# Attention scores formed a second time, already turned, with one reciprocal of the sum for a pair of heads

## The reference

```python
scale, shift = split(cond @ W_emb + b_emb)        # one row per batch
xn  = rms_norm(x) * g_norm * (1 + scale) + shift
q, k, v = split(xn @ W_qkv)                       # 16 heads of 64
q, k = rms_norm(q) * g_q, rms_norm(k) * g_k       # over the 64 of a head
attn = softmax(q @ k.T * 64 ** -0.5)              # 512 x 512 per head
o = attn @ v
out = x + o + o @ W_out
```

## Time and profile before

| what | value |
|---|---|
| median of three runs | 2278.25 us |
| the profiled execution | 2278.89 us |
| its span | 2276.0 us |
| TensorE busy | 2256.2 us (99%) |
| VectorE busy | 1597.9 us (70%) |
| ScalarE busy | 1345.7 us (59%) |
| GpSimd busy | 651.7 us (29%) |
| granted TensorE clock | 0.999 |

### The profile page before, as it was taken

One profiled execution on the slowest core, in us unless ns is written; L12 is line 12 of the kernel. 1 busy time (PEld: TensorE's weight loads), 2 busy tenths in 40 slices (PEclk: granted clock), 3 DMA queues, 4 the chain that ended last, 5 costly groups with the idle time before them and its releaser, 6 DMA issues.

```text
span 2276.0 us, 36733 instructions
## 1 busy us (share of the span) xinstructions
PE 2256.2 (99%) x13392; PEld 2110.3 (93%) x13392; DVE 1597.9 (70%) x3284; ACT 1345.7 (59%) x3101; POOL 651.7 (29%) x880
## 2 busy tenths in 40 slices
PE   8999999999999999999999999999999999999999
PEld 4999989999999999999999999999999999999999
DVE  4898784787827778287872878738786487854875
ACT  4687772667616676176762667526674366743663
POOL 3444431324213241122312234122331223302220
PEclk9999999999999999999999999999999999999999
DMA  9544346422364332733236332362323723246331
GB/s 359 224 167 177 112 154 228 178 99 110 118 220 184 107 115 88 256 148 112 111 114 256 112 112 112 122 253 107 112 112 130 291 92 118 82 151 246 111 121 65
DMA packets 71269, 346.35 MB, mean 152 GB/s; under 512 B 7601, under 2 KB 43441, under 8 KB 47537
## 3 DMA queue, kind: packets, MB, share of 16 engines
q1 hardware_dynamic: 71088, 344.01, 41.2%
HBM read 293.65 MB, written 50.33 MB: 151 GB/s over the span
## 4 chain that ended last, share of the span: by engine, by line
PE 86%; DVE 8%; ACT 2%; issue 1%; POOL 0%; DMA 0%; ACTq 0%; DVEq 0%
PE proj_bank L502 18%; PE proj_bank L500 18%; PE proj_bank L501 18%; PE flip_bank L598 9%; PE pv_bank L609 5%; PE pv_bank L610 5%; PE score_bank L590 4%; PE score_bank L591 4%; PE flip_bank L553 2%; DVE probs L865 2%; DVE neg_max L859 2%; DVE pt_lo L869 2%; PE flip_bank L563 1%; ACT k_hi L700 1%; PE proj_bank L525 1%
## 5 line engine op out<-in xcount | busy, mean ns | idle before, releaser
L500 PE MATMUL proj_bank<-w_split,xn_hi 128*128 128x384 f32 x2048 | 700.0, 342 | 1.4 <-DVE res L907 0.8
L502 PE MATMUL proj_bank<-w_split,xn_lo 128*128 128x384 f32 x2048 | 688.5, 336 | 0.0
L501 PE MATMUL proj_bank<-w_split,xn_hi 128*128 128x384 f32 x2048 | 687.4, 336 | 0.0
L718 ACT ACTIVATE probs<-score_bank,neg_max 128x512 f32<-128x512 f32 x512 | 352.6, 691 | 213.5 <-DVE neg_max L859 211.2
L500 PEld LDWEIGHTS proj_bank<-w_split,xn_hi 128*128 128x128 f32 x2048 | 385.2, 188 | 18.1 <-DVE xn_lo L854 1.0
L501 PEld LDWEIGHTS proj_bank<-w_split,xn_hi 128*128 128x128 f32 x2048 | 385.5, 188 | 15.2
L724 ACT CAST pt_hi<-flip_bank 128x512 fp32r<-128x512 f32 x512 | 288.8, 591 | 182.0 <-PE flip_bank L598 91.1
L869 DVE TENSOR_TENSOR pt_lo<-flip_bank,pt_hi 128x512 fp32r<-128x512 f32 x512 | 339.9, 685 | 78.1 <-ACT pt_hi L724 75.9
L502 PEld LDWEIGHTS proj_bank<-w_split,xn_lo 128*128 128x128 f32 x2048 | 384.8, 188 | 0.0
L859 DVE TENSOR_REDUCE neg_max<-score_bank 128x1 f32<-128x512 f32 x512 | 341.3, 684 | 17.0 <-PE score_bank L591 13.0
L865 DVE TENSOR_SCALAR probs<-probs,row_inv 128x512 f32<-128x512 f32 x512 | 275.7, 539 | 18.1
(11 more groups left out here) (86 smaller groups left out, 3205.1 us busy)
## 6 DMA issues: line engine op xcount, KB each, us to landing
w_split<-w_store SPq DMA_DIRECT2D x140, 1536.0 KB, 7.0
w_store<-w_split SPq DMA_DIRECT2D x20, 1536.0 KB, 10.1
x_tile<-in_x SPq DMA_DIRECT2D x32, 512.0 KB, 11.0
w_raw<-in_w_qkv SPq DMA_DIRECT2D x16, 768.0 KB, 8.4
w_split<-w_store SPq DMA_DIRECT2D x12, 1024.0 KB, 5.1
w_raw<-in_x SPq DMA_DIRECT2D x56, 192.0 KB, 6.7
out<-w_raw SPq DMA_DIRECT2D x56, 192.0 KB, 1.9
emb_stage<-in_w_emb SPq DMA_DIRECT2D x5, 1024.0 KB, 10.6
```

The source lines that it names most:

```text
L500: nc.tensor.matmul(dst, a_hi, w_hi, start=(kt == 0), stop=False)
L501: nc.tensor.matmul(dst, a_hi, w_lo, start=False, stop=False)
L502: mm = nc.tensor.matmul(dst, a_lo, w_hi, start=False, stop=(kt == KT - 1))
L718: nc.scalar.activation(probs[h][:, i, :], score_bank[n % 2][:, :], ACT.Exp, bias=neg_max[:, n:n + 1], accum_out=row_sum[:, n:n + 1]).then_ ...
```

## The change

The probabilities are no longer turned. Once the maxima of a head's rows are known, the scores are formed again with keys on the rows and queries on the columns (`F`), and the exponential is taken from that bank. The maximum of a query is now a value per column, so it is subtracted inside the product: `H` turns the 128x4 maxima with one transpose, VectorE spreads them over a diagonal of four rows in `q_max` (below the head's high part of q, which the new step `Z` copies there), and four rows of `k_lo` are set to one. The first scores (`S`), which serve for the maxima alone, lose their second matmul.

The exponential is written unscaled to `probs`, `E` copies its high part and `F` on VectorE subtracts it, both from SBUF. The sum of a column is over keys, that is over rows: GpSimd adds the four tiles of a head (`U`, three additions), ScalarE and VectorE bring the two heads together (`U`, `N`), `J` splits the sum, and `G` multiplies it with a matrix of ones. ScalarE takes the logarithm and the exponential of its negative, and VectorE scales the pair's result with this inverse and one Newton step. The flip banks now have one release counter for each engine that frees them. Three pairs are started early instead of two, and the first batch has two residual tiles instead of three. All five orders are new.

```diff
-LATE = 2
+LATE = 3
 HEAD, BODY, TAIL: all lists new; TensorE's part around pair 7 in BODY, for instance:
+        6F5 6W3 6F6 6F7 6W4 7T0 7T1 6W5 8C8 8C9 8C10 8C11 7S0 7S1 6W6 8C12 6W7 7S2 8C13 8C14 7S3 8C15 7H0 7S4 7S5 9C0
+        7F0 7F1 9C1 7S6 7S7 7F2 6G0 9C2 7H1 9C3 7W0 7W1 7F3 9C4 9C5 7F4 7F5 7W2 7W3 7F6 7F7 9C6 8T0 7W4 8T1 7W5 9C7 9C8
 ...and VectorE's:
+        6O0 7S1 6O1 8M2 7S2 7S3 6N0 7H0 6N1 8D3 7S4 7S5 6J0 8M3 7S6 7S7 7F0 7F1 6G0 7H1 9D0 7F2 7F3 7F4 7F5 7O0 9M0 8T0
 TensorE
                     elif kind == "S":
-                        pe.wait_ge(exp_done, it * 8 + (n - 2 + 1 + CREDIT))
+                        wait_past(pe, max_done, it * 8 + (n - 1))
...
-                        nc.tensor.matmul(score_bank[n % 2][:, :], q_t, k_hi[h][:, :], start=True, stop=False)
-                        nc.tensor.matmul(score_bank[n % 2][:, :], q_t, k_lo[h][:, :], start=False,
-                                         stop=True).then_inc(score_full, 1)
+                        nc.tensor.matmul(score_bank[n % 2][:, :], q_split[:, h, i * P:(i + 1) * P], k_hi[h][:, :],
+                                         start=True, stop=True).then_inc(score_full, 1)
+                    elif kind == "H":
+                        flip_wait(pe, u)
+                        pe.wait_ge(max_done, it * 8 + 4 * n + 4)
+                        nc.tensor.transpose(flip_bank[flip][0:TT, 0:P], neg_max[:, 4 * n:4 * n + 4],
+                                            ident[:, :]).then_inc(flip_full, 1)
                     elif kind == "F":
-                        for qt in range(TT):
-                            mm = nc.tensor.transpose(flip_bank[flip][:, qt * P:(qt + 1) * P],
-                                                     probs[h][:, qt, i * P:(i + 1) * P], ident[:, :])
+                        if i == 0:
+                            freed(pe, "H", h, it)
+                            freed(pe, "T", 1, it)
+                            pe.wait_ge(q_copied, it + 1)
+                        nc.tensor.matmul(flip_bank[flip][:, :], k_hi[h][:, i * P:(i + 1) * P], q_split[:, h, :],
+                                         start=True, stop=False)
+                        nc.tensor.matmul(flip_bank[flip][:, :], k_lo[h][:, i * P:(i + 1) * P], q_max[:, h, :],
+                                         start=False, stop=True).then_inc(flip_full, 1)
+                    elif kind == "G":
+                        pe.wait_ge(sum_lo_done, it + 1)
+                        nc.tensor.matmul(flip_bank[flip][:, :], head_ones[:, :], sum_hi, start=True, stop=False)
+                        nc.tensor.matmul(flip_bank[flip][:, :], head_ones[:, :], sum_lo, start=False,
+                                         stop=True).then_inc(flip_full, 1)
 ScalarE
+                    elif kind == "Z":
+                        for head in range(2):
+                            op = nc.scalar.copy(q_max[rows(head), head, :], f32(q_split[rows(head), head, :]))
+                    elif kind == "G":
+                        nc.scalar.activation(sum_inv, flip_bank[flip][:, :], ACT.Ln).then_inc(ln_done, 1)
+                        act.wait_ge(ln_done, it + 1)
+                        nc.scalar.activation(sum_inv, sum_inv, ACT.Exp, scale=-1.0).then_inc(inv_done, 1)
-                        nc.scalar.activation(probs[h][:, i, :], score_bank[n % 2][:, :], ACT.Exp,
-                                             bias=neg_max[:, n:n + 1],
-                                             accum_out=row_sum[:, n:n + 1]).then_inc(exp_done, 1)
                     elif kind == "F":
+                        nc.scalar.activation(probs[h][:, i, :], flip_bank[flip][:, :],
+                                             ACT.Exp).then_inc(flip_freed["ScalarE"], 1)
+                    elif kind == "E":
+                        nc.scalar.copy(pt_hi[n % 2][:, :], probs[h][:, i, :]).then_inc(p_hi_done, 1)
+                    elif kind == "U":
+                        nc.scalar.copy(key_moved[mine, :], probs[n][other, 3, :]).then_inc(keys_moved, 1)
+                    elif kind == "J":
+                        nc.scalar.copy(sum_hi, key_sum).then_inc(sum_hi_done, 1)
 VectorE
+                    elif kind == "H":
+                        nc.vector.tensor_tensor(q_max[at:at + TT, n, :].rearrange("p (t q) -> p t q", q=P),
+                                                flip_bank[flip][0:TT, 0:P].unsqueeze(1).to_broadcast([TT, TT, P]),
+                                                ident[0:TT, 0:TT].unsqueeze(2).to_broadcast([TT, TT, P]),
+                                                ALU.mult).then_inc(flip_freed["VectorE"], 1)
+                    elif kind == "F":
+                        nc.vector.tensor_tensor(pt_lo[n % 2][:, :], probs[h][:, i, :], f32(pt_hi[n % 2][:, :]),
+                                                ALU.subtract).then_inc(p_lo_done, 1)
                     elif kind == "N":
-                        nc.vector.reciprocal(row_inv[:, n:n + 1], row_sum[:, n:n + 1]).then_inc(inv_done, 1)
-                        nc.vector.tensor_scalar(probs[h][:, i, :], probs[h][:, i, :], row_inv[:, n:n + 1], None,
-                                                ALU.mult).then_inc(probs_ready, 1)
+                        nc.vector.tensor_tensor(key_sum[mine, :], probs[n][mine, 3, :], key_moved[mine, :],
+                                                ALU.add).then_inc(key_sum_done, 1)
+                    elif kind == "J":
+                        nc.vector.tensor_tensor(sum_lo, key_sum, f32(sum_hi), ALU.subtract).then_inc(sum_lo_done, 1)
+                    elif kind == "G":
+                        nc.vector.tensor_tensor(sum_times_inv, flip_bank[flip][:, :], sum_inv,
+                                                ALU.mult).then_inc(flip_freed["VectorE"], 1)
+                        nc.vector.scalar_tensor_tensor(o_pair[:, :], o_pair[:, :], -1.0, sum_inv, ALU.mult,
+                                                       ALU.mult).then_inc(o_scaled, 1)
+                        nc.vector.scalar_tensor_tensor(o_pair[:, :], sum_times_inv, -2.0, o_pair[:, :], ALU.add,
+                                                       ALU.mult).then_inc(o_norm_done, 1)
 GpSimd, three additions for each head as they come ready
+            def add_keys(it, n):
+                head, part = n // 3, n % 3
...
+                op = nc.gpsimd.tensor_tensor(e[:, dst, :], e[:, src, :], e[:, dst, :], ALU.add)
 tiles
-        first_res = [sb(f"res{i}", [P, QKV]) for i in range(3)]
+        first_res = [sb(f"res{i}", [P, QKV]) for i in range(2)]
```

More of the change, by code:

```diff
@@ L41 @@
[L41 to L45, removed]
@@ L226, in flip_buf, with order_of, flip_table @@
-def flip_buf(order, kind, n, p):
-    places = HEAD_FLIPS if order is HEAD else TAIL_FLIPS if order is TAIL else BODY_FLIPS
-    before = 0 if order is HEAD else HEAD_FLIPS[1]
-    assert BODY_FLIPS[1] % 2 == 0
-    return (before + places[0][(kind, n, p)][0]) % 2
-FIRST_X = {HEAD_FLIPS[0][("X", r, 0)][0] for r in range(TT)}
-def releases(order, u):
-    return u if order is HEAD and u - 2 in FIRST_X else u - 1
+def order_of(b):
+    return HEAD if b == 0 else TAIL if b == B - 1 else BODY
+def flip_table():
+    table, releases, counts = {}, [], {"ScalarE": 0, "VectorE": 0}
+    for b in range(B):
+        for step in order_of(b)["TensorE"]:
+            p, d, kind, n = read_step(step)
+            if kind in "TFXHG":
+                table[(kind, n, b + d if kind == "X" else b * PAIRS + p)] = len(releases)
+                for owner in ("VectorE", "ScalarE") if kind == "X" else ("ScalarE",) if kind == "F" else ("VectorE",):
+                    counts[owner] += 1
+                    releases.append((owner, counts[owner]))
+    return table, releases
@@ L243, in is_first @@
+FLIPS, RELEASES = flip_table()
 def is_first(b):
@@ L333, in cond_attention @@
         v_stage = sb("v_stage", [P, 2, TT, P])
-        q_split = [sb(f"q_split{h}", [P, T], F32R) for h in range(2)]
+        q_split = sb("q_split", [P, 2, T], F32R)
+        q_max = sb("q_max", [P, 2, T], F32R)
         k_hi = [sb(f"k_hi{h}", [P, T], F32R) for h in range(2)]
@@ L337, in cond_attention @@
         v_split = [sb(f"v_split{h}", [P, TT, P], F32R) for h in range(2)]
-        probs = [sb(f"probs{h}", [P, TT, T]) for h in range(2)]
+        probs = [sb("probs0", [P, TT, T])]
+        with nc.sbuf_tensor("sum_split", [P, TT, T], F32R) as sum_split:
+            pass
+        probs.append(sb("probs1", [P, TT, T]))
         pt_hi = [sb(f"pt_hi{i}", [P, T], F32R) for i in range(2)]
@@ L557, in cycle @@
                         for half in range(2):
-                            wait_past(pe, flip_free, releases(order, u + half))
+                            flip_wait(pe, u + half)
                             if half == 0:
@@ L721, in cycle @@
                     elif kind == "F":
                         act.wait_ge(flip_full, u + 1)
[L723 to L724 removed]
+                        if i == 0 and not is_first(it):
```

(17 more changed lines are left out.)

445 lines of the change are left out of this document (238 added, 207 removed).

## The result

| | before | after |
|---|---|---|
| median | 2278.01 us | 2401.78 us |
| the profiled execution's span | 2276.0 us | 2397.6 us |
| granted TensorE clock | 0.999 | 0.992 |

The ratio is 1.054, with a 95% interval from 1.053 to 1.056: the changed kernel is 124 us slower, where 35 us faster was forecast. The forecast was wrong, outside its range.

A forecast was written before the change was run, and what follows sets the result against it. The prediction took TensorE, busy 99% of the span, as the bound, so the span is the sum of what it issues. -63 + 14 + 6 + 5 + 3 = -35 us gave 2243 us, range 2216 to 2275 us.

The forecast's parts named there:

- the rival of the reloaded tables: If the logarithm needs another set, each pair has two table loads in `G`'s chain: 2357 us, chance 6%.
- The forecast case without reloads: Whole kernel: TensorE's saving less some waits gives 2243 us; the case, 2225 to 2262 us, had 64%.
- TensorE's own work: TensorE's matmuls and transposes, gained and lost in `S`, `F`, `G` and `H`, sum to -63 us.
- the sum of the waits: Waits that reach TensorE in four places: 14, 6, 5 and 3 us.
- Middle and later batches: 57 pairs: blocked VectorE operations exceed the spare time behind the maxima and before `F3`, 0.25 us per pair, 14 us.
- First batch: VectorE, nearly full there, becomes the bound for some pairs: 6 us, between 0 and 15.
- End of the first batch with two residual tiles: Tile 9 waits for a later load, tiles 10 and 11 load one and two round trips later: 5 us, 0 to 10.
- The end: The last pair's new chain, about 13 us, against about 11 us of other TensorE work: 3 us, between 0 and 5.
- The lock at the maxima: GpSimd's additions block VectorE in nearly every pair, late to `H` and `G`'s bank: 115 us, 2344 us in all, chance 10%.
- Other engines: Busy sums outside TensorE, none the bound: VectorE near 1760 us, ScalarE 1521 us, GpSimd near 1160 us.

The follow-up runs named there:

- experiment 1: The changed kernel with one activation table set holding both logarithm and exponential, loaded once at ScalarE's start: 2303.95 us, ratio 1.011 to the kernel before.
- experiment 7: experiment 1 without the Newton step, one multiplication in place of three VectorE operations, ScalarE's logarithm freeing the bank: 2302.55 us, ratio 1.011.
- experiments 1 and 4: experiment 1, and the same with GpSimd's additions cut to 4 of 512 columns: 2303.95 us and 2286.71 us.
- experiments 5 to 10: experiment 1 with steps moved, 2312.02 us; kernel before with reloads, 2349.94; no Newton step, whole or 4-column sums, 2302.55, 2286.60; copy or subtraction cut, 2293.92, 2283.91.

## Why the prediction was wrong

- **The step that failed: the rival of the reloaded tables, at 6%.** Its mechanism and place were right: two loads in `G`'s chain for each pair, the held bank, TensorE behind it. Its size was 2 us per pair, 128 us less 14; measured are 98 us, 1.5 us per pair. The forecast's own sum had no term for it: what failed was the chance. Nothing in the trace of before spoke against it, and I leaned on a rule. The Trainium skill, in "ScalarE activation tables: per-element evaluation and per-set limits", section "Table sets in the compiler and the runtime", has the loads placed per block by the greedy longest run. I took that to mean one set for the whole loop; the trace has 129 loads, so that reading does not hold for this kernel. The Trainium skill, in "ScalarE: Activation LUTs", section "Table sets: the hidden batching unit", counts one load for a logarithm followed by an exponential; it came true only in the experiments that load that set by its number, and the changed kernel itself has two loads for the two functions.
- **The forecast case without reloads, 2243 us: measured 2304 us.** Its size was off too, by 61 us. TensorE's own work was right: by the second sum it fell from 2213 to 2152 us, by 61 us where 63 were forecast. The single terms agree. `S`, by the starts of its matmuls, went from 248.2 to 132.9 us (-115.3, forecast -118.5), `G` takes 32.5 us (forecast 29.6), and an `H` 0.03 us from its start to the next one's and 0.08 on the interval behind it, the 0.11 that I had taken. So the step that failed in this case is the sum of the waits: +28 us forecast, +88 measured (112 less 24).
- **The waits of TensorE, by place.** Of the 88 us, 70 stand ahead of a step (87 less 17) and 18 inside steps, for which the forecast had no term. About 8 of these 18 are on the interval right behind a stall, 0.1 us longer than the typical one in `F` and `W`, 3 at the lower clock, and the other 7 are spread in small pieces. The 70:
  - Middle and later batches: 14 forecast, about 45 measured (49.8 and 3.9, less 8.4 and 0.1). This is the term that was mis-sized most. I had looked at the place behind the maxima, and the waits for `q_max` are small (2.6 us in experiment 1). The largest stalls are before the products `6W2` and `6W4` (16.6 us), where VectorE has `+X3 8D1` ahead of the subtractions, and at `3T0` (4.4 us); the rest is spread over many steps. I found the tight place by reading two spots of the lists and never went through those where x is turned.
  - First batch: 6 forecast; about 20 measured besides its end (33.2 less 8.2 and 5). And its cause was not the one named: VectorE with 73 us less in all changes it by 2 us (experiment 7).
  - End of the first batch with two residual tiles: 5 forecast, 5.0 measured. The chain of the changed kernel, which answers to the earlier trace rows, has the second round trip:
```profile
413.61 5.14 DMA out<-res
...
419.14 4.52 DMA out<-res
423.68 8.32 DMA res<-in_x
...
432.10 0.44 DVE res L988
```
  - The end: 3 forecast, 1.3 measured before `P3` in experiment 1 (2.6 after).
- **The lock at the maxima, at 10%,** was wrong in size. The subtraction is blocked as forecast, but what reaches TensorE from all of GpSimd's additions is 17 to 19 us, and not 115. VectorE itself loses 1.5 us per pair (1730.0 less 1636.2 us busy in experiments 1 and 4, over 64), where 2.6 were forecast.
- **Other engines:** ScalarE with one table has 1531.5 us (forecast 1521). The exponential out of a bank, without a bias from a tile and without the accumulator, takes 598 ns, not 691 and 200. That the sum is right within 11 us is luck: 512 exponentials are 48 us shorter, which I had not counted, and the accumulator's read had begun 0.11 us before the exponential's end, so that 56 of its 102 us were never ScalarE's to save.

So the 124 us are: 98 for the reloads, 17 for GpSimd's additions, 70 for other stalls, less 61 of TensorE's work. That the 70 come from the orders is what experiments 5 to 10 leave over. It is not shown directly, and their cause stays open, since no order without them was found; my one try moved the stalls on. No version here beats the kernel before; of those that leave nothing out the best is experiment 1, 1.1% slower.

## What to carry to other kernels

Before a second transcendental function goes into a loop, ask which table sets will be loaded, count the loads in the first trace, and load the joint set by its number if there is one. A change that takes work from the bounding engine and gives more, smaller meetings to the others must be priced by its orders and not by sums: here, with one table, 61 us of work saved stood against 88 us of stalls, with no engine but TensorE over 75% busy. When a stall is left, thin one engine's operation to a few columns; if that takes away a sixth of the engine's work and brings back a quarter of the stalls or less (20 us of 88), its fullness is not the main cause.

## What was unexpected

- A table set that holds both functions exists and loads in the same 1283 ns, yet 128 loads were placed in turn, one before each change of function.
- A load costs its 1.28 us and hardly more: ScalarE is idle 1.1 us in all before the 64 loads of each line, and the activation starts 0.02 us behind its load, as the timeline of the changed kernel has it.
```profile
999.93 1.28 ACT L747 ACT_TABLE_LOAD   x1
1001.23 0.63 ACT L747 ACTIVATE probs<-probs 128x512 f32<-128x512 f32 x1
```
- VectorE's reciprocal of 128x512 takes 3350 ns, although that of one column takes 158 and a multiplication of two such tiles some 0.7 us. That is what logarithm, exponential and Newton step together avoid, and only with one table do they avoid it.
